# Layer 0's attention: a head's keys transposed by VectorE in 32x32 blocks and by SBUF-to-SBUF transfers, in place of TensorE transposes

## The reference, cut to what matters

```
qkv = silu(hidden_states @ qkv_w.T)                  # q, k, v of each head, 1024 x 128
scores    = einsum('bhnd,bhmd->bhnm', cq, ck) * diag_decay
intra     = einsum('bhnm,bhmd->bhnd', scores, cv)
inter     = einsum('bhnd,bhde->bhne', cq * q_decay, kv)
kv_next   = kv * block_decay + einsum('bhnd,bhne->bhde', ck * k_decay, cv)
...
return gate * normed @ out_w.T
```

## Time and profile before

| | |
|---|---|
| median of three runs | 3272.53 us |
| lowest and highest | 3272.32 and 3273.12 us |
| span of the profiled execution, first to last instruction | 3270.4 us |
| what lies around the span, by the median | 2.1 us |
| mean granted TensorE clock over the span | 0.993 |
| layer 0's attention, about | 0 to 1180 us |
| period of one head in its loop | 35.85 us |

### The profile page before, as it was taken

The page is one execution under the profiler, slowest core; times in us unless marked ns, Lnnn a source line. Parts: engine busy times, 40 slices in busy tenths (PEclk is TensorE's granted clock), DMA queues, the critical chain, the costliest instruction groups (busy, mean ns, idle before and its releaser), DMA issues. The chain is left out here.

```text
span 3270.4 us, 58692 instructions
## 1 busy us (share of the span) xinstructions
PE 3188.5 (97%) x19936; PEld 2909.5 (89%) x19936; DVE 2034.0 (62%) x3413; ACT 1389.1 (42%) x2375; POOL 971.0 (30%) x819
## 2 busy tenths in 40 slices
PE   8999999999999978999999999999999999997998
PEld 8989999998999857999999999999999999996786
DVE  3444444444444457777777777777777777777555
ACT  3333333333333322555555555555555555553221
POOL 3333333333333332222222222222222222211765
PEclk9999999999999989999999999999999999999999
DMA  3111111111111001000000000000000000002551
GB/s 115 40 44 40 35 45 41 37 39 45 40 35 45 29 23 34 31 17 31 15 30 15 30 15 30 15 30 15 30 15 30 20 26 29 16 7 78 158 140 55
DMA packets 102601, 128.50 MB, mean 39 GB/s; under 512 B 7297, under 2 KB 66705, under 8 KB 102417
## 3 DMA queue, kind: packets, MB, share of 16 engines
q1 hardware_dynamic: 101696, 126.96, 12.5%
q10 hardware_dynamic: 816, 0.79, 0.1%
q0 software_dynamic: 32, 0.02, 0.0%
HBM read 125.63 MB, written 2.10 MB: 39 GB/s over the span
## 5 line engine op out<-in xcount | busy, mean ns | idle before, releaser
L1287 ACT ACTIVATE b_prob<-b_s_ps,b_shift,b_rstd 128x1024 f32<-128x1024 f32 x252 | 304.2, 1207 | 580.7 <-DVE b_shift L1449 580.7
L1447 DVE TENSOR_REDUCE b_row_max<-b_s_ps 128x1 f32<-128x1024 f32 x252 | 307.2, 1219 | 78.6 <-PE b_s_ps L84 78.5
L82 PE MATMUL b_pj_kq<-b_w_hi,xT_hi 128*128 128x384 f32 x1008 | 341.6, 339 | 1.2 <-DVE b_nat L1417 1.2
L84 PE MATMUL b_pj_kq<-b_w_hi,xT_lo 128*128 128x384 f32 x1008 | 342.1, 339 | 0.0
L83 PE MATMUL b_pj_kq<-b_w_lo,xT_hi 128*128 128x384 f32 x1008 | 341.5, 339 | 0.0
L488 ACT ACTIVATE a_sig<-a_pj 128x512 f32<-128x512 f32 x192 | 114.9, 598 | 498.3 <-PE a_pj L84 498.3
L82 PE MATMUL a_pj<-b_w_hi,xT_hi 128*128 128x256 f32 x1024 | 300.0, 293 | 11.2 <-DVE xT_lo L639 11.1
L84 PE MATMUL a_pj<-b_w_hi,xT_lo 128*128 128x256 f32 x1024 | 290.4, 284 | 0.0
L83 PE MATMUL a_pj<-b_w_lo,xT_hi 128*128 128x256 f32 x1024 | 288.8, 282 | 0.0
L1219 POOL TENSOR_TENSOR b_rstd<-b_mean_sq,power 128x4 f32<-128x4 f32 x128 | 128.9, 1007 | 528.3 <-DVE b_mean_sq L1427 525.0
L1373 PE MATMUL b_t_ps<-ident,b_prob 128*128 128x128 f32 x2048 | 265.6, 273 | 4.8 <-ACT b_prob L1287 4.5
(11 more groups left out here) (273 smaller groups left out, 9126.6 us busy)
## 6 DMA issues: line engine op xcount, KB each, us to landing
b_w_raw<-in_w SPq DMA_DIRECT2D x32, 768.0 KB, 4.3
b_w_raw<-in_w SPq DMA_DIRECT2D x95, 256.0 KB, 3.1
a_w_raw<-in_w SPq DMA_DIRECT2D x32, 256.0 KB, 2.7
a_ow_raw<-in_ow SPq DMA_DIRECT2D x32, 256.0 KB, 3.0
b_ow_raw<-in_ow SPq DMA_DIRECT2D x32, 256.0 KB, 4.5
m_raw_w<-in_mlp_w SPq DMA_DIRECT2D x28, 256.0 KB, 3.0
m_raw_z<-in_mlp_z SPq DMA_DIRECT2D x28, 256.0 KB, 3.8
m_raw_s<-in_mlp_s SPq DMA_DIRECT2D x28, 256.0 KB, 4.9
```

What stands on the lines that cost most here:

```text
L82: pe.matmul(out, w_hi, x_hi, start=first, stop=False)
L84: return pe.matmul(out, w_lo, x_hi, start=False, stop=last)
L1287: act.activation(prob[:, :], score_banks(h, t)[:, :], ACT.Exp, bias=shift[:, t:t + 1], scale=rstd[b][:, t, 1:2], accum_out=row_sum[:, t:t ...
L1447: dve.tensor_reduce(row_max[:, t:t + 1], score_banks(h, t)[:, :], AX_X, ALU.max).then_inc(max_done, 1)
```

## The change

The two `tk` banks, `transposes`, `copy_k` and their semaphores go. VectorE gets `block_k`: after stage 4's `silu_half`, in the step before the one that needs them, one instruction transposes each 32x32 block of the head's keys in place of its block, from `kv_nat` into a new buffer `k_blocks` (128 x 8 x 128). SyncE gets `move_k`: sixteen DMAs, one for each pair of a quarter r of the partitions and a quarter c of the columns, carry the blocks to their places in `k_T`. Each moves 32 partitions x 8 chunks x 32 elements, so 256 pieces of 128 bytes, 32 KB in all. They stand in SyncE's stream behind the query weights of head h and ahead of its gate weights, for head h-2; for the last two heads they follow their output weights. `scores` waits for all sixteen (`k_moved`) in place of ScalarE's copy. `block_k` waits for the moves of the head before. The scratch memory of DMAs issued by GpSimd is set to 1024 bytes.

```
+    BLK = 32
+    GROUPS = P // BLK
+    MOVED = 16 * GROUPS * GROUPS
...
+        k_blocks = sb("k_blocks", [P, NT, HD])
...
-        tk = [bank(f"tk{j}", [P, HALF]) for j in range(2)]
...
+            def move_k(g):
+
+                sp.wait_ge(k_blocked, g + 1)
+                to = k_T[:, :].rearrange("p (t n) -> p t n", t=NT)
+                for c in range(GROUPS):
+                    for r in range(GROUPS):
+                        sp.dma_start(to[c * BLK:(c + 1) * BLK, :, r * BLK:(r + 1) * BLK],
+                                     k_blocks[r * BLK:(r + 1) * BLK, :, c * BLK:(c + 1) * BLK]).then_inc(k_moved, 16)
+
             def load(h, b):
...
                 load_weights(h, 2)
+                move_k(h - 2)
                 load_weights(h, 3)
...
             load_output_weights(HEADS - 2)
+            move_k(HEADS - 2)
             load_decays(HEADS - 1, 1)
             load_output_weights(HEADS - 1)
+            move_k(HEADS - 1)
...
-            def copy_k(h, b, j):
-
-                act.wait_ge(k_tr, 2 * h + j + 1)
-                wait(act, scored, 2 * (h - 1) + j + 1)
-                act.activation(k_T[:, j * HALF:(j + 1) * HALF], tk[j][:, :], ACT.Copy).then_inc(k_T_done, 1)
...
-                            copy_k(h, b, s // 2)
                             decay_k(h, b, s // 2)
...
-            def transposes(h, b, j):
-                pe.wait_ge(silu, 6 * h + 2 * j + 2)
-                wait(pe, k_T_done, 2 * (h - 1) + j + 1)
-                for c in range(CH):
-                    last = pe.transpose(tk[j][:, c * CHUNK:(c + 1) * CHUNK], kv_nat[b][:, j * CH + c, 0:HD],
-                                        sh.ident[:, :])
-                last.then_inc(k_tr, 1)
...
             def scores(h, b, j):
-                pe.wait_ge(k_T_done, 2 * h + j + 1)
+                pe.wait_ge(k_moved, MOVED * (h + 1))
                 pe.wait_ge(silu, 6 * h + 6)
...
-                        if s in (0, 2):
-                            transposes(h, b, s // 2)
...
+            def block_k(g, bg):
+
+                dve.wait_ge(silu, 6 * g + 4)
+                wait(dve, k_moved, MOVED * g)
+                dve.transpose(k_blocks[:, :, :], kv_nat[bg][:, :, 0:HD]).then_inc(k_blocked, 1)
...
                     if project and s < GATE.start:
                         silu_half(h + 1, 1 - b, s)
+                    if project and s == KV.stop:
+                        block_k(h + 1, 1 - b)
                     if output:
                         add_output(h - 1, s)
...
-    nc = bacc.Bacc("TRN2", target_bir_lowering=False, num_devices=1)
+    nc = bacc.Bacc("TRN2", target_bir_lowering=False, num_devices=1, dynamic_dma_scratch_size=1024)
```

More of the change, by code:

```diff
@@ L279, in l0_attention @@
         silu = sem("silu")
-        k_tr = sem("k_tr")
-        k_T_done = sem("k_T_done")
+        k_blocked = sem("k_blocked")
+        k_moved = sem("k_moved")
         k_decayed = sem("k_decayed")
```

## The result

The changed kernel takes 3371.19 us (median of four runs, 3369.38 to 3372.63) against 3272.82 us before: a ratio of 1.0299, with a 95% interval from 1.0284 to 1.0314. It is slower by 98 us. The forecast was 3303 us, with a range from 3250 to 3370. The side was right; the size was a third of what came, and the time lies just above the range.

A forecast was written before the change was run, and what follows sets the result against it. TensorE, busy throughout the loop, was taken as the bound: 3270.4 us, less 27.5 for transposes, plus 58.3 of stall waiting for the moves, gives 3301.2, and with 2.1 from span to median 3303 us; range 3250 to 3370.

The forecast's parts named there:

- The saving: TensorE, start of each head: removing two groups of four transposes saves 0.43 us a group, 27.5 us over 32 heads.
- VectorE, GpSimd's scratch memory, the loads behind the moves: VectorE's added transpose (1.2 to 2.35 us), smaller scratch memory and slightly later SyncE loads: all covered, nothing on the path.
- Where the moves start and when they are due: SyncE's order sets the first transfer at 813.57; TensorE needs the keys at its scores, 822.79.
- the window: Time from the first transfer's issue on SyncE to TensorE's scores in a head: 9.22 us.
- I, the distance of two issues: SyncE, sixteen moves a head: successive issues 0.57 us apart, with 0.47 and 0.65 kept as bounds.
- the dear row: Earlier trace's loads with four 512-byte pieces in each of 128 partitions, issued 0.65 us apart; used as upper bound.
- L: Time from the last move's issue to its landing: 2.4 us, bounds 2.1 and 3.1.
- The stall in sum: TensorE waiting at the scores: 28 heads at 1.73 us, head 0 6.2, head 1 3.7, together 58.3 us.
- my "dear rate" case: SyncE issues 0.65 us apart, landing 2.7 us: 3348 us; upper end of the forecast's own case, chance 0.55.
- The cheap rate: Rival: SyncE issues the moves every 0.47 us, so the kernel gets faster, 3251 to 3265 us; chance 0.27.
- The dear packets: Rival: 128-byte packets cost far more than their size, so DMA engines set the pace; 3618 us at 80 ns; chance 0.08.

The follow-up runs named there:

- the last run: Changed kernel with its sixteen 32 KB moves read from HBM, one piece of 1024 bytes in each of 32 partitions: 3255.45 us.

## Why the prediction was wrong

**The saving** was right: 0.86 us a head forecast, 0.89 measured by the moves put first.

**VectorE, GpSimd's scratch memory, the loads behind the moves**: costed at nothing, and nothing they were.

**Where the moves start and when they are due** was right in mechanism: SyncE's order, not the blocks, sets the start, and the wait ends in the moves' landing. The first issue comes 0.61 us behind the query load's (810.13 to 810.74) instead of the 0.79 that I had from a gap at another place, so the window is 9.40 us instead of 9.22.

**I, the distance of two issues, failed.** I took 0.57 us, between two rows, and it was 0.66 as the mean of a block, the dear end of the earlier trace rows. Over fifteen distances that is 1.35 us a head. The reasoning behind it was wrong as well: I had sought the price in the number and the form of the pieces. All the rows I drew on were loads from HBM, and none had both ends in SBUF, which the last run, set beside the one with long pieces, shows to be what counts for these moves. That the dear row had nearly the right figure I count as luck: it was a load from HBM in 512-byte pieces, and the moves cost as much without short pieces.

**L** was taken as 2.4 us. From the last issue, 820.64, to the scores, 822.83, it is 2.19, of which 1.97 are the landing. Together: 9.90 + 2.19 - 9.40 = 2.69 us, and 2.67 are measured, against a forecast of 1.73.

**The stall in sum**: 26 heads at 2.67 make 69 us, heads 1 to 3 12.6 (5.4, 3.6, 3.6), head 0 7.3 (its scores start at 46.51 instead of 39.64, with 0.43 saved): 89 us, where the sum had 58.3. The sum gave heads 2 and 3 the steady stall and head 1 only 3.7 us; it didn't know that the blocks of these heads take 11.5 us.

```profile
46.51 2.08 PE L564 MATMUL a_s_ps<-a_q_T,a_k_T 128*128 128x128 f32 x8 [6.81 <-DMA a_k_T<-a_k_blocks]
```

**The step that was missing is TensorE's clock.** The sum took a stall for a delay that leaves the work behind it as it was. The clock fell behind the stall in 21 of 29 heads, 1.5 us each, and with 0.1 us of restart in every head and some 1.5 us in head 0 that is about 36 us. None of the forecast's cases had this term; with it, my "dear rate" case at 3348 us would have reached past 3370 and the range with it.

The account of the changed kernel: 32 x 0.89 = 28.5 us saved, 89 us of stall, 36 us of slow clock and restart, 96.5 us in all; the two spans differ by 97.2 us.

**The rivals.** The cheap rate, to which I gave 0.27, did not come; 0.48 us came only in the run whose moves read from HBM. The dear packets did not come either. The DMA table of the changed kernel from 815 to 820 us, where only the moves are in flight, has:

```profile
DMA packets 1981, 0.24 MB, mean 48 GB/s; under 512 B 1981, under 2 KB 1981, under 8 KB 1981
...
q1 hardware_dynamic: 1981, 0.24, 32.3%
```

That is 0.323 x 16 x 5 us / 1981 = 13 ns a packet, half of the 26.5 ns of a 512-byte one, so 0.21 us of each engine's time in a transfer. The transfers landed 2.0 us after their issue (median), those of 256 short pieces hardly later than those of 32 long ones (1.8). This agrees with what the forecast cited from the Trainium skill ("DMA: Bandwidth & Descriptors", Why small descriptors are slow) on traffic from SBUF to SBUF; a penalty below 512 bytes, if there is one, is too small to matter here.

## What to carry to other kernels

When work moves from a bound engine to transfers, count the issues, not the bytes: their number times the distance of two issues, plus one landing, must fit between the place in the queue where they stand and the moment they are due. If they don't fit, look first at what stands ahead of them in that queue for no need of theirs; here one line moved up turned 98 us of loss into 20 us of gain. And price a stall of TensorE twice, once as time and once for the clock behind it; in these runs the second price came in some heads once TensorE had idled for about 1.9 us or more, and in none after 1.2 us.

## What the runs showed of the hardware

- A DMA issued by SyncE right behind another took 0.64 to 0.66 us from SBUF to SBUF, whether it had 256 pieces of 128 bytes, 128 of them, or 32 of 1024, over 32 or 128 partitions (blocks of sixteen between 10.1 and 10.6 us in the steady heads), and 0.48 us from HBM to SBUF with one piece of 1024 bytes in each of 32 partitions (7.57 us, one execution). What in the issuing makes the difference was not tried.
- Behind its stalls TensorE's granted clock fell to 0.50 in 21 of 29 heads and stayed at 1.00 in the other 8; in the 26 steady heads it had idled for 2.5 us each time. With 2.3 us of idle time it fell in 2 of the 26 (heads 4 and 20), with 1.9 to 2.0 us in 6, with 1.2 us in none. It stayed at 1.00 behind one idle time of 3.4 us (head 3), and fell behind one of 1.9 us (head 2 with fourteen moves). Filling the wait with useless matmuls kept it at 1.00.
- A DMA packet of 128 bytes between two places in SBUF took 13 ns, one of 512 bytes from HBM 26.5 ns.
- VectorE's block transpose of 128x1024 float32 elements from SBUF to SBUF took 1.23 us each time, 1.2 ns a column, where a product of two such operands took mostly 2.26.
